# Attention and channel-mix block on one core: the shift of the softmax transposed by DMA, four operand buffers, and the turns of input and attention in 64-row tiles with one copy

## The chip, the cores and the metric

The kernel runs on one core of a Trainium2 chip. The metric is device microseconds of one execution, the median of several runs. TensorE (PE in the rows) multiplies and transposes, VectorE (DVE), ScalarE (ACT) and GpSimd (POOL) do the elementwise work, and SyncE (SP) issues all DMAs, in the order of its program.

## What is computed

Input x is (32, 256, 128) fp32. For each of 32 batches:

```python
xn = layernorm(x)
q, k, v = xn @ wq + bq, xn @ wk + bk, xn @ wv + bv      # 16 heads of 8
att = softmax(q @ k.T / sqrt(8)) @ v                    # per head, 256 x 256 scores
xp = xn shifted down one token, zeros first
r = sigmoid((mu_r*xn + (1-mu_r)*xp) @ W_r)
k2 = square(relu((mu_k*xn + (1-mu_k)*xp) @ W_k))
y = x + att.reshape(256, 128) @ wo.T + bo + r * (k2 @ W_v)
```

## The kernel before

A batch is one step t; its 16 heads are 16 units u. A step of the program works on several batches at once: the layernorm of batch t+4 and t+3, the projections of t+3, the spill of t+2, the maxima of t+1, the exponentials of t, and the output of t-1. `live(d)` says that batch t+d exists, `n(d)` is the count that a semaphore has when batch t+d is done. Each engine has its own program in order of time, and semaphores tie them. The steps 4 to 27 are a loop of 4 steps a pass (`LOOP`), the rest is straight code.

The scores are made twice from split operands. q and k are cut into three bf16 parts (h, m, l), written to DRAM (`spill`) and read back as `ops`, where 48 rows hold 6 products of parts. Rows 0 to 63 and 64 to 127 of `ops` hold different heads (r = 0, 1), so that TensorE runs two matmuls at once, in two tiles of 64 rows. The first time (line 717) VectorE takes the maximum of each row from the bank (line 557); the second time (line 707) three more rows of `ops` (51 in all) carry the negated maximum in three bf16 parts against ones, so that the bank holds score minus maximum and ScalarE takes the exponential (line 454). Line 717 runs two units ahead (`LEAD`): at unit 14 it starts with batch t+2. A bank for exponentials is free again two units later.

The way of the maximum, the *shift*, for each half of the heads: GpSimd splits it into three parts (`split_max`, lines 332 to 339), TensorE transposes them (`transpose_shift`, line 639: half 1 in unit 1 of its own step, half 0 of batch t+1 in unit 9), ScalarE copies them from PSUM (`move_shift`, line 424), SyncE copies them into `ops` (`load_shift`, line 257). Half 0 is needed at unit 0, half 1 at unit 8.

After the units 1, 5, 9 and 13 stand 16 value matmuls in four column tiles (`mix_values`, line 631). After the other odd units stand full fp32 matmuls: unit 3 the gate (736) and the transposes of the mixed values (747), from which VectorE takes the reciprocals (567) and `att` (570); unit 7 the channel mix (758), the transposes of xn (768) and of att (773), which ScalarE copies to `xn_t` (472) and, with the bias bv added, to `att_t` (476); unit 11 the values (646), the hidden layer (792) and the output projection (799); unit 15 the projections K and Q (665, 673). Two banks, `misc[0]` and `misc[1]`, take turns in all of these as `near` and `far`. VectorE adds the gate to the channel mix at line 584; GpSimd adds ffn and x (`rest`, line 376) and the output (407).

SyncE's step: load x of batch t+4, `load_ops` half 1 of t+1, spill h, `load_shift` half 1, spill m and l, `load_ops` half 0 of t+2 when the scores of unit 7 have been read, `load_shift` half 0, store y of t-1. `ops` has two buffers.

## Time and profile before

| | |
|---|---|
| median of 3 runs | 468.71 us (468.67 to 470.33) |
| the profiled execution | 468.32 us, its span 466.2 us |
| busy share | PE 96%, DVE 86%, ACT 85%, POOL 79%, weight loads (PEld) 59% |
| DMA engines | 45% of the span, 60.4 MB |
| mean granted TensorE clock | 0.971; 1.00 (2.4 GHz) in each stretch read from 40 us on, 0.50 to 0.60 from 14 to 40 us |

The span runs from the first to the last instruction; the execution's own time has some 2 us around it. The times of the rows below are microseconds from the span's start. PE is a matmul or transpose, PEld a weight load; an fp32 matmul is two passes and so two instructions, a transpose is one. The length of a TensorE row includes the way through the array, so that starts, not ends, show its pace.

### The profile page before, as it was taken

What the parts mean: (1) busy time and instruction counts of PE and PEld (TensorE: products, weight loads), DVE (VectorE), ACT (ScalarE), POOL (GpSimd) and SP (SyncE); (2) the same over time, 40 slices, a digit from 0 to 9 for tenths busy, and PEclk for the clock granted to TensorE, in tenths of its full rate; (3) what the DMA queues carried; (4) which work ended last, traced back from release to release, by engine and by line L of the source; (5) the groups of instructions that cost most, each with busy time, mean ns of one, the idle gap of its engine ahead of it and who ended that gap; (6) DMA issues with size and microseconds to landing.
All of it is one profiled execution on the core that took longest, in us unless ns stands there. A gap on an engine that the chain in (4) does not pass through costs nothing.

```text
span 466.2 us, 15769 instructions
## 1 busy us (share of the span) xinstructions
PE 449.2 (96%) x5254; PEld 275.1 (59%) x5254; DVE 400.7 (86%) x824; ACT 394.1 (85%) x896; POOL 366.5 (79%) x674
## 2 busy tenths in 40 slices
PE   6689999999999999999999999999999999999996
PEld 5245666666656666556665666566656666666554
DVE  7578999999988999899999999899998999989831
ACT  2138899999988999989998999989998999989894
POOL 6667888888888988888888888888888888887321
PEclk9558999999999999999999999999999999999999
DMA  4533465545345545344554544355545444455100
GB/s 135 158 116 99 124 162 148 142 134 150 109 140 148 157 127 155 108 132 130 148 159 129 156 139 127 104 147 155 159 137 138 136 126 125 137 151 147 51 15 24
DMA packets 86061, 60.43 MB, mean 130 GB/s; under 512 B 6224, under 2 KB 73808, under 8 KB 86032
## 3 DMA queue, kind: packets, MB, share of 16 engines
q1 hardware_dynamic: 86032, 60.06, 45.0%
q8 instruction: 17, 0.28, 0.3%
q14 instruction: 12, 0.10, 0.1%
HBM read 29.89 MB, written 29.36 MB: 127 GB/s over the span
## 4 chain that ended last, share of the span: by engine, by line
PE 88%; DMA 3%; issue 2%; DVE 2%; ACT 2%; SPq 1%; ACTq 0%; DVEq 0%; POOL 0%
PE bank_val L631 26%; PE bank_exp L707 18%; PE bank_max L717 11%; PE misc L736 5%; PE misc L758 4%; PE misc L646 4%; PE misc L665 3%; PE misc L747 3%; PE misc L799 3%; PE misc L792 3%; PE misc L673 2%; PE misc L773 2%; PE misc L768 1%; DMA ops<-spill 1%; DVE neg_max L557 1%
## 5 line engine op out<-in xcount | busy, mean ns | idle before, releaser
L557 DVE TENSOR_REDUCE neg_max<-bank_max 128x2 f32<-128x512 f32 x512 | 327.9, 684 | 37.9 <-PE bank_max L717 32.8
L454 ACT ACTIVATE probs<-bank_exp 128x512 f32<-128x512 f32 x504 | 273.5, 597 | 27.4 <-PE bank_exp L707 25.3
L717 PE MATMUL bank_max<-ops 48*128 48x256 bf16 x1024 | 161.5, 278 | 0.0
L707 PE MATMUL bank_exp<-ops 51*128 51x256 bf16 x1008 | 156.0, 273 | 4.2 <-issue 2.1
L631 PE MATMUL bank_val<-probs,val 128*25 128x256 f32 x2048 | 136.8, 385 | 0.8 <-ACT probs L454 0.8
L707 PEld LDWEIGHTS bank_exp<-ops 51*128 51x128 bf16 x1008 | 74.7, 95 | 66.2 <-issue 51.5
L631 PEld LDWEIGHTS bank_val<-probs,val 128*25 128x25 f32 x2048 | 50.5, 103 | 52.2 <-issue 27.0
L717 PEld LDWEIGHTS bank_max<-ops 48*128 48x128 bf16 x1024 | 77.0, 96 | 5.7
L356 POOL TENSOR_SCALAR xn<-x_in,moments,rstd 128x128 f32<-128x128 f32 x62 | 49.3, 802 | 0.0
L395 POOL TENSOR_TENSOR mixed_x<-mixed_x,xn_t 128x512 f32<-128x512 f32 x32 | 40.7, 1273 | 2.5
L370 POOL TENSOR_TENSOR qk_l<-qk_rest,qk_m 128x512 bf16<-128x512 f32 x31 | 36.0, 1163 | 2.5
L523 DVE SCALAR_TENSOR_TENSOR qk_rest<-misc,col,qk_h 128x256 f32<-128x256 f32 x64 | 30.6, 479 | 6.2 <-ACT qk_h L436 6.2
L391 POOL TENSOR_TENSOR mixed_x<-dx,col 128x512 f32<-128x512 f32 x32 | 33.4, 1042 | 2.5
L436 ACT ACTIVATE qk_h<-misc,col 128x256 bf16<-128x256 f32 x64 | 27.2, 480 | 8.9 <-PE misc L665 7.0
L407 POOL TENSOR_TENSOR y<-projected,rest 128x256 f32<-128x256 f32 x31 | 22.6, 729 | 14.2 <-ACT projected L491 14.2
L366 POOL TENSOR_TENSOR act_sq<-act_r 128x256 f32<-128x256 f32 x32 | 19.6, 613 | 17.0 <-DVE qk_rest L523 17.0
L424 ACT COPY shift<-misc 24x256 bf16<-24x256 bf16 x64 | 23.2, 362 | 9.1 <-PE misc L639 2.5
L351 POOL TENSOR_TENSOR x_bo<-x_in,bo_all 128x256 f32<-128x256 f32 x32 | 23.2, 726 | 4.1 <-issue 3.9
L402 POOL TENSOR_TENSOR rstd<-var_eps,minus_half 128x2 f32<-128x2 f32 x32 | 22.8, 712 | 2.5
L646 PE MATMUL misc<-w,xn_t 128*128 128x128 f32 x128 | 23.1, 304 | 1.3 <-DVE qk_rest L523 1.3
L665 PE MATMUL misc<-xn_t,w 128*128 128x256 f32 x64 | 23.4, 449 | 1.0 <-ACT xn_t L472 1.0
L472 ACT COPY xn_t<-misc 128x256 f32<-128x256 f32 x32 | 12.0, 374 | 14.0 <-PE misc L768 13.9
(77 smaller groups left out, 627.9 us busy)
## 6 DMA issues: line engine op xcount, KB each, us to landing
ops<-spill SPq DMA_DIRECT2D x126, 192.0 KB, 3.4
spill<-qk_h SPq DMA_DIRECT2D x64, 192.0 KB, 3.3
spill<-qk_m SPq DMA_DIRECT2D x64, 128.0 KB, 1.9
x_in<-x SPq DMA_DIRECT2D x32, 128.0 KB, 2.2
spill<-qk_l SPq DMA_DIRECT2D x32, 128.0 KB, 1.8
y_out<-y SPq DMA_DIRECT2D x32, 128.0 KB, 1.9
ops<-shift SPq DMA_DIRECT2D x128, 6.0 KB
w<-weights SPq DMA_DIRECT2D x1, 448.0 KB, 3.0
```

Source lines behind the costliest of these rows:

```text
L356: last = nc.gpsimd.tensor_scalar(xn[:, i, :], x_in[(c + 3) % TURN][:, i, :], moments[:, i, 0:1], rstd[:, i:i + 1], ALU.subtract, ALU.mult)
L370: nc.gpsimd.tensor_tensor(qk_l[:, :, :], qk_rest[:, :, :], qk_m[:, :, :], ALU.subtract).then_inc(l_done, 1)
L391: nc.gpsimd.tensor_tensor(mix[:, :, :], dx[:, :].unsqueeze(1).broadcast_to([P, 2, S]), col[:, C_MUR:C_MUK + 1].unsqueeze(2).broadcast_to([ ...
L395: nc.gpsimd.tensor_tensor(mix[:, :, :], mix[:, :, :], prev.unsqueeze(1).broadcast_to([P, 2, S]), ALU.add).then_inc(mix_tokens_done, 1)
L454: nc.scalar.activation(probs[g % 2][:, u % G, :, :], exp_bank(u, live)[:, :, :], ACT.Exp, scale=SCALE).then_inc(exp_done[u], 1)
L523: nc.vector.scalar_tensor_tensor(out=qk_rest[:, a, :], in0=bank[:, 0:S], scalar=col[:, C_BQ + a:C_BQ + a + 1], in1=qk_h[:, a, :], op0=ALU. ...
L557: nc.vector.tensor_reduce(out=neg_max[hf][:, :, r, pr], in_=bank_max[MAX_BANK[v]][:, :, :], axis=AX_X, op=ALU.max, negate=True).then_inc(m ...
L631: last = nc.tensor.matmul(bank_val[SW * j:SW * j + MW, g // 2, :], weights[:, 0:MW] if fresh else weights[:, VW:VW + MW], probs[g % 2][:, ...
L646: last = nc.tensor.matmul(bank[:, i * D:(i + 1) * D], xn_t[c % TURN][:, 1 + i * P:1 + (i + 1) * P], w[:, W_V, :], start=True, stop=True)
L665: nc.tensor.matmul(far[:, 0:S], w[:, W_K, :], moving, start=True, stop=True).then_inc(qk_psum[1], 1)
L707: exp_mm = nc.tensor.matmul(exp_bank(u, live)[:, i, :], ops[p][rows, hf, 1, pr, i * P:(i + 1) * P], ops[p][rows, hf, 0, pr, :], start=True ...
L717: max_mm = nc.tensor.matmul(bank_max[MAX_BANK[v]][:, i, :], of[rows, max_hf, 0, max_pr, i * P:(i + 1) * P], of[rows, max_hf, 1, max_pr, :] ...
```

## The change

- **Shift.** `max_parts` becomes 128 columns wide, with zeros behind the 24 that are used. SyncE transposes it by a DMA transpose into `shift` (`transpose_shift`), and copies the 24 rows that count into `ops` as before. TensorE's line 639 and ScalarE's line 424 go. GpSimd's split of half 0 moves ahead of `rest` (line 376).
- **Operand buffers.** `ops` has four buffers instead of two. Both halves of batch t+2 are loaded in step t, half 0 after the transpose of the shift of half 0, half 1 after the copy of that shift. The ones of the two new buffers are copied by DMA from the first (`copy_ones`). 
- **SyncE's order.** Transpose of half 1, spill h, shift of half 1, spill m and l, transpose of half 0, ops half 0, shift of half 0, ops half 1, and last the load of x (of batch t+5) and the store of y.
- **Turns.** xn and att are transposed in tiles of 64 rows: eight transposes with 64 columns in place of four with 128, the upper rows into bank 0 of `misc` and the lower into bank 1, all in the columns S to 2S. The wait for `att_done`, which stood before the transposes of att, stands before the last matmul of line 758. One ScalarE copy of 128x512 takes both results into `xn_t`, which has twice the columns; `att_t` is its second half.
- **Bias.** bv is no longer added to `att_t`; one matmul at the start forms bv @ wo and VectorE adds it to bo.
- **Loop.** The loop covers steps 4 to 23.

The diff, cut to its core (left out: the declarations of semaphores, the bias, and waits that only follow the renaming of `misc`):

```diff
-LOOP = (1, 7)
+LOOP = (1, 6)
...
-        xn_t = [sb(f"xn_t{i}", [P, 1 + S]) for i in range(TURN)]
+
+        xn_t = [sb(f"xn_t{i}", [P, 1 + 2 * S]) for i in range(TURN)]
...
-        ops = [sb(f"ops{i}", [P, 2, 2, PR, S], BF16) for i in range(2)]
+        ops = [sb(f"ops{i}", [P, 2, 2, PR, S], BF16) for i in range(TURN)]
...
-        max_parts = [sb(f"max_parts{i}", [P, ST, 2, 3, PR], BF16) for i in range(2)]
-        shift = [sb(f"shift{i}", [2 * 3 * PR, S], BF16) for i in range(2)]
...
+        max_parts = [sb(f"max_parts{i}", [P, ST, P], BF16) for i in range(2)]
+        shift = [sb(f"shift{i}", [P, ST, P], BF16) for i in range(2)]
...
-        misc = [psum(f"misc{i}", [P, 2 * S]) for i in range(2)]
+
+        misc = psum("misc", [P, 2, 2 * S])
...
+            def copy_ones():
+
+                sp.wait_ge(k_filled[0], 1)
+                for i in range(2, TURN):
+                    for r in range(2):
+                        rows = slice(RG * r + KS, RG * r + KE)
+                        sp.dma_start(ops[i][rows, :, 1], ops[0][rows, :, 1]).then_inc(ones_in, 16)
...
-            def load_shift(half, p, count, before):
-
-                after(sp, shift_done[half], count)
...
+            def transpose_shift(half, count, before):
+                sp.wait_ge(parts_zero, 1)
+                sp.wait_ge(max_split[half], count)
+                after(sp, shift_in[half], before)
+                sp.dma_start_transpose(shift[half][:, :, :], max_parts[half][:, :, :].rearrange("p n c -> p (n c)")).then_inc(
+                    shift_done[half], 16)
+
+            def load_shift(half, c, done, before):
+
+                sp.wait_ge(shift_done[half], done)
                 after(sp, shift_in[half], before)
                 for r in range(2):
-                    sp.dma_start(ops[p][RG * r + KS:RG * r + KE, half, 0],
-                                 shift[half][3 * PR * r:3 * PR * (r + 1), :]).then_inc(shift_in[half], 16)
+                    sp.dma_start(ops[c][RG * r + KS:RG * r + KE, half, 0],
+                                 shift[half][3 * PR * r:3 * PR * (r + 1), :, :]).then_inc(shift_in[half], 16)
...
             def step(t, c, n, moved, paired, quad, live):
                 p = c % 2
-                if live(4) and live(0):
-
-                    sp.wait_ge(x_bo_done, n(0))
-                    sp.wait_ge(xn_done, n(0))
-                    load_x(t + 4, c)
-                if live(1):
-
-                    after(sp, exp_scores[H - 1], n(-1))
-                    load_ops(1, 1 - p, moved(1, SPILLS), moved(0, 2))
+                if live(0):
+                    transpose_shift(1, n(0), moved(-1, 2))
                 if live(2):
...
-                    load_shift(1, p, n(0), moved(-1, 2))
+                    load_shift(1, c, moved(0, 1), moved(-1, 2))
                 if live(2):
                     spill_part(p, "m", qk_m, (m_done, m_done), n)
                     spill_l(p, n)
-
-                    after(sp, exp_scores[HALF - 1], n(0))
+                if live(1):
+                    transpose_shift(0, n(1), moved(0, 2))
+                if live(2):
+
+                    after(sp, exp_scores[H - 1], n(-1))
                     if not live(0):
                         sp.wait_ge(k_filled[p], 1)
                     if live(1):
-                        load_ops(0, p, moved(2, SPILLS), moved(1, 2))
+                        load_ops(0, (c + 2) % TURN, moved(2, SPILLS), moved(1, 2))
                     else:
-                        load_first_ops(p, moved(2, SPILLS))
+                        load_first_ops((c + 2) % TURN, moved(2, SPILLS))
                 if live(1):
-                    load_shift(0, 1 - p, n(1), moved(0, 2))
+                    load_shift(0, (c + 1) % TURN, moved(1, 1), moved(0, 2))
+                if live(2):
+                    load_ops(1, (c + 2) % TURN, moved(2, SPILLS), moved(1, 2))
+                if live(1) and not live(0):
+                    copy_ones()
+                if live(5) and live(1):
+                    sp.wait_ge(x_bo_done, n(1))
+                    sp.wait_ge(xn_done, n(1))
+                    load_x(t + 5, (c + 1) % TURN)
                 if live(-1):
-
-                    sp.wait_ge(y_done, n(-1))
-                    sp.dma_start(out_dram[t - 1], y[1 - p][:, :].rearrange("p (n d) -> p n d", n=ST)).then_inc(
-                        out_done[1 - p], 16)
-
-            steps(sp, step, (2, SPILLS))
+                    store_y(t - 1, 1 - p, n(-1))
+
+            steps(sp, step, (1, 2, SPILLS))
...
                                             ALU.subtract).then_inc(l_done, 1)
+                if live(1):
+                    split_max(0, n(1), moved(0, 1))
                 if live(-1):
                     pool.wait_ge(ffn_done, n(-1))
                     after(pool, y_done, n(-3))
...
-            def move_shift(half, bank, count, before):
-                act.wait_ge(shift_psum[half], count)
-                after(act, shift_in[half], before)
-                nc.scalar.copy(shift[half][:, :], shift_in_bank(bank)).then_inc(shift_done[half], 1)
...
-                    if u == 1 and live(0):
-                        move_shift(1, near, n(0), moved(-1, 2))
...
-                        move_values(p, far, n(2))
-                    if u == 7 and live(3):
-                        act.wait_ge(xn_t_psum, n(3))
-                        nc.scalar.copy(xn_t[(c + 3) % TURN][:, 1:1 + S], near[:, S:2 * S]).then_inc(xn_t_done, 1)
-                    if u == 7 and live(-1):
-                        act.wait_ge(att_t_psum, n(-1))
-                        after(act, wo_psum, n(-2))
-                        nc.scalar.activation(att_t[:, :], far[:, 0:S], ACT.Identity,
-                                             bias=col[:, C_BV:C_BV + 1]).then_inc(att_t_done, 1)
-                    if u == 9 and live(1):
-                        move_shift(0, far, n(1), moved(0, 2))
+
+                        for r in range(2):
+                            act.wait_ge(xn_t_psum[r], n(3))
+                        move_values(p, near, n(2))
+                    if u == 7 and (live(3) or live(-1)):
+                        turned = xn_t[(c + 3) % TURN]
+
+                        after(act, ffn_psum, n(0))
+                        for r in range(2):
+                            after(act, xn_t_psum[r], n(3))
+                            after(act, att_t_psum[r], n(-1))
+
+                        cols = slice(0 if live(3) else S, 2 * S if live(-1) else S)
+                        nc.scalar.copy(turned[:, 1 + cols.start:1 + cols.stop].rearrange("p (n r c) -> p r n c", r=2, c=RG),
+                                       misc[:, :, S + cols.start // 2:S + cols.stop // 2].rearrange(
+                                           "p r (n c) -> p r n c", c=RG)).then_inc(xn_t_done if live(3) else att_t_done, 1)
...
-            def transpose_shift(half, bank):
-                for st in range(ST):
-                    last = nc.tensor.transpose(shift_in_bank(bank)[:, st * P:(st + 1) * P],
-                                               max_parts[half][:, st].rearrange("p r j k -> p (r j k)"),
-                                               ident16[:, :])
-                last.then_inc(shift_psum[half], 1)
...
-                    if u == 1 and live(0):
-                        pe.wait_ge(max_split[1], n(0))
+                    if u == 3 and live(0):
                         pe.wait_ge(act_r_done, n(0))
                         after(pe, qk_rest_done[1], n(2))
-                        transpose_shift(1, near)
-                    if u == 3 and live(0):
-                        pe.wait_ge(shift_done[1], n(0))
...
                     if u == 5 and live(0):
                         mix_values(0, n(0), n(-1), p)
+                    if u == 7 and live(2) and not live(1):
+                        pe.wait_ge(qk_rest_done[1], n(2))
+                        project_values(c + 2, near)
+                    if u == 7 and live(3):
+                        pe.wait_ge(xn_done, n(3))
+                        after(pe, qk_rest_done[0], n(2))
+                        after(pe, qk_rest_done[1], n(2))
                     if u == 7 and live(0):
                         pe.wait_ge(act_sq_done, n(0))
                         pe.wait_ge(gate_done, n(0))
                         for i in range(ST):
+                            if i == ST - 1:
+
+                                after(pe, att_done, n(-1))
                             last = nc.tensor.matmul(near[:, i * D:(i + 1) * D], act_sq[:, i * P:(i + 1) * P],
                                                     w[:, W_VV, :], start=True, stop=True)
                         last.then_inc(ffn_psum, 1)
-                    if u == 7 and live(2) and not live(1):
-                        pe.wait_ge(qk_rest_done[0], n(2))
-                        project_values(c + 2, far)
                     if u == 7 and live(3):
-                        pe.wait_ge(xn_done, n(3))
-                        after(pe, qk_rest_done[1], n(2))
                         for i in range(ST):
-                            last = nc.tensor.transpose(near[:, S + i * P:S + (i + 1) * P], xn[:, i, :], ident[:, :])
-                        last.then_inc(xn_t_psum, 1)
+                            for r in range(2):
+                                rows, k = slice(RG * r, RG * (r + 1)), S + i * RG
+                                last = nc.tensor.transpose(misc[:, r, k:k + RG], xn[rows, i, :], ident[rows, rows])
+                                if i == ST - 1:
+                                    last.then_inc(xn_t_psum[r], 1)
                     if u == 7 and live(-1):
-                        pe.wait_ge(att_done, n(-1))
+                        if not live(0):
+                            pe.wait_ge(att_done, n(-1))
                         for st in range(ST):
-                            last = nc.tensor.transpose(far[:, st * P:(st + 1) * P],
-                                                       att[:, st * H:(st + 1) * H].rearrange("p k e -> p (k e)"),
-                                                       ident[:, :])
-                        last.then_inc(att_t_psum, 1)
+                            for r in range(2):
+                                rows, k = slice(RG * r, RG * (r + 1)), S + (ST + st) * RG
+                                last = nc.tensor.transpose(misc[:, r, k:k + RG],
+                                                           att[rows, st * H:(st + 1) * H].rearrange("p k e -> p (k e)"),
+                                                           ident[rows, rows])
+                                if st == ST - 1:
+                                    last.then_inc(att_t_psum[r], 1)
                         if not live(0):
                             keep_running(2)
                     if u == 9 and live(0):
                         mix_values(1, n(0), n(-1), p)
-                    if u == 9 and live(1):
-                        pe.wait_ge(max_split[0], n(1))
-                        after(pe, att_t_done, n(-1))
+                    if u == 11 and live(1) and live(0):
+                        if live(3):
+                            pe.wait_ge(xn_t_done, n(3))
+                        elif live(-1):
+                            pe.wait_ge(att_t_done, n(-1) - (B - TURN))
                         after(pe, qk_rest_done[0], n(2))
-                        if not live(0):
-                            pe.wait_ge(consts_made, 2)
```

## Rows read from the trace of the kernel before

**Rows 1.** Page, chain that ended last: shares of the span by engine.
```profile
PE 88%; DMA 3%; issue 2%; DVE 2%; ACT 2%; SPq 1%; ACTq 0%; DVEq 0%; POOL 0%
```

**Rows 2.** Stretch; busy us of PE, PEld, DVE, ACT, POOL; clock, DMA share, GB/s.
```profile
200.00:213.26 13.26, 13.26 (x165) 8.27 (x164) 12.05 (x26) 12.21 (x29) 11.45 (x21) 1.00 0.52 146
```

**Rows 3.** TensorE in order of time: start us, us, engine, line, operation, tiles, count.
```profile
200.71 0.28 PE L707 MATMUL bank_exp<-ops 51*128 51x256 bf16 x1
...
201.25 1.07 PE L631 MATMUL bank_val<-probs,val 128*25 128x256 f32 x16
...
202.34 0.28 PE L707 MATMUL bank_exp<-ops 51*128 51x256 bf16 x1
...
204.95 1.06 PE L631 MATMUL bank_val<-probs,val 128*25 128x256 f32 x16
205.95 0.28 PE L707 MATMUL bank_exp<-ops 51*128 51x256 bf16 x1
...
212.89 0.71 PE L758 MATMUL misc<-w,act_sq 128*128 128x128 f32 x4
213.44 0.38 PE L768 MATMUL misc<-ident,xn 128*128 128x128 f32 x2
213.66 0.38 PE L773 MATMUL misc<-ident,att 128*128 128x128 f32 x2
213.97 0.28 PE L707 MATMUL bank_exp<-ops 51*128 51x256 bf16 x1
```

**Rows 4.** VectorE in order of time, same batch.
```profile
206.41 1.29 DVE L557 TENSOR_REDUCE neg_max<-bank_max 128x2 f32<-128x512 f32 x2 [0.25 <-PE bank_max L717]
207.86 0.48 DVE L523 SCALAR_TENSOR_TENSOR qk_rest<-misc,col,qk_h 128x256 f32<-128x256 f32 x1 [0.16 <-ACT qk_h L436]
...
209.84 2.71 DVE L557 TENSOR_REDUCE neg_max<-bank_max 128x2 f32<-128x512 f32 x4
212.47 0.35 DVE L567 RECIPROCAL inv_den<-misc 128x32 f32<-128x32 f32 x1
212.86 0.42 DVE L570 TENSOR_TENSOR att<-misc,inv_den 128x256 f32<-128x256 f32 x1
```

**Rows 5.** Groups of instructions by form: busy, mean ns.
```profile
L454 ACT ACTIVATE probs<-bank_exp 128x512 f32<-128x512 f32 x504 | 273.5, 597 | 27.4 <-PE bank_exp L707 25.3
...
L639 PE MATMUL misc<-ident,max_parts 128*24 128x128 bf16 x128 | 17.8, 221 | 0.0
...
L758 PEld LDWEIGHTS misc<-w,act_sq 128*128 128x128 f32 x128 | 16.7, 190 | 6.7 <-issue 6.7
...
L768 PEld LDWEIGHTS misc<-ident,xn 128*128 128x128 f32 x64 | 8.2, 148 | 1.5 <-DVE xn L531 0.8 <-issue 0.4 <-POOL xn L356 0.3
```

**Rows 6.** All engines near the end of the span, in order of time.
```profile
461.16 0.42 DVE L570 TENSOR_TENSOR att<-misc,inv_den 128x256 f32<-128x256 f32 x1
461.64 0.20 PEld L773 LDWEIGHTS misc<-ident,att 128*128 128x128 f32 x2 [0.21 <-DVE att L570]
```

**Rows 7.** ScalarE in order of time, units 7 to 9.
```profile
213.86 0.37 ACT L472 COPY xn_t<-misc 128x256 f32<-128x256 f32 x1
214.13 0.48 ACT L476 ACTIVATE att_t<-misc,col 128x256 f32<-128x256 f32 x1
214.49 1.09 ACT L454 ACTIVATE probs<-bank_exp 128x512 f32<-128x512 f32 x2
```

**Rows 8.** GpSimd in order of time: the last step of a split.
```profile
207.13 0.22 POOL L339 TENSOR_TENSOR max_parts<-max_rest,max_parts 128x16 bf16<-128x16 f32 x1
```

**Rows 9.** SyncE's DMA issues in order of time.
```profile
209.68 1.53 SPq L257 DMA_DIRECT2D ops<-shift  x2
...
214.33 0.80 SPq L242 DMA_DIRECT2D ops<-spill  x2
```

**Rows 10.** Page, DMA issues: KB each, median us from issue to landing.
```profile
ops<-spill SPq DMA_DIRECT2D x126, 192.0 KB, 3.4
...
spill<-qk_l SPq DMA_DIRECT2D x32, 128.0 KB, 1.8
```

More of the change, by code:

```diff
@@ L327, in split_max @@
                 m, zero = neg_max[half], zeros[:, :, :, :]
-                part = [max_parts[half][:, :, :, j, :] for j in range(3)]
+                parts = max_parts[half][:, :, 0:2 * 3 * PR].rearrange("p n (r j k) -> p n r j k", r=2, j=3)
+                part = [parts[:, :, :, j, :] for j in range(3)]
                 last_unit = HALF * (half + 1) - 1
                 after(pool, max_done[last_unit], count)
-                after(pool, shift_psum[half], before)
+                after(pool, shift_done[half], before)
                 nc.gpsimd.tensor_tensor(part[0], m[:, :, :, :], zero, ALU.add).then_inc(max_h[half], 1)
@@ L440, in step @@
                 p = c % 2
-                near, far = misc[p], misc[1 - p]
+                near, far = misc[:, p, :], misc[:, 1 - p, :]
                 if live(2):
@@ L502, in _ @@
             nc.vector.memset(zeros[:, :, :, :], 0.0)
+            for i in range(2):
+                last = nc.vector.memset(max_parts[i][:, :, :], 0.0)
+            last.then_inc(parts_zero, 1)
             nc.vector.memset(eps[:, :], EPS)
@@ L613, in _ @@
             for _ in range(WARM):
-                nc.tensor.matmul(misc[0][:, 0:P], ident[:, :], ident[:, :], start=True, stop=True)
+                nc.tensor.matmul(misc[:, 0, 0:P], ident[:, :], ident[:, :], start=True, stop=True)
             def keep_running(count):
@@ L676, in step @@
                 p = c % 2
-                near, far = misc[p], misc[1 - p]
+                near, far = misc[:, p, :], misc[:, 1 - p, :]
                 for u in range(H):
```

89 lines of the change are left out of this document (51 added, 38 removed).

## Prediction

> **What bounds the kernel now.** I read the chain of waits first: 88% of it is TensorE's [rows 1]. Then one steady batch (200.71 to 213.97 us, 13.26 us, as the others of the loop body): TensorE is busy without a hole, VectorE for 12.05 us and ScalarE for 12.21 us of it [rows 2]. So TensorE's order of work is the period, and a batch has only 1.2 us in which VectorE is idle: whatever is taken from TensorE helps up to there and no further, and whatever new wait ties TensorE to VectorE costs at once.
>
> Third, TensorE in order of time [rows 3]. Three things are to be seen. (a) The bf16 shift transposes, two per half, are cheap: 16 value matmuls start at 201.25, two transposes follow, the next score matmuls start at 202.34, 1.09 us later; where none stand between (204.95 to 205.95) it is 1.00. A pair of them costs 0.09 us. (b) The block at the end of unit 7 (line 758, then 768 and 773) runs from 212.89 to 213.97. Two transposes start in 0.22 (213.44, 213.66), so one each 0.11 us; four 758 passes in 0.55, so they stream from 213.00 on, after a load of 0.11. (c) Two units of scores are four starts of 0.11, but take 0.54 to the next block (200.71 to 201.25): 0.10 goes into the change of tile size, and with the load that can't be made ahead it is 0.20 before line 758. Going back is 0.09 (213.66 and two transposes of 0.11 end at 213.88; the scores start at 213.97).
>
> Fourth, VectorE beside it [rows 4]. From its reduce at 206.41 VectorE is busy, but for 0.16 us, till att is written at 212.86+0.42 = 213.28 us. That chain begins with the scores of unit 14 (TensorE, 205.95) and everything in it is VectorE's own work. TensorE's first transpose of att starts at 213.66, so today att is ready 0.3 us early.
>
> **The change, part by part.**
>
> *Shift transposes leave TensorE* (line 639: 128 in all, 4 a batch [rows 5]). Two pairs of 0.09 us. The pair in unit 1 stands between unit 14 and unit 7, where, as the next part shows, TensorE will wait for VectorE anyway: worth nothing then. The pair in unit 9 is worth 0.09 us.
>
> *The wait for att_done moves ahead of the last 758 matmul.* The new transposes write columns S and up of both banks of misc, also those that VectorE still reads for att; so the wait stands before the matmul of i=1 and thus before its weight load. Today that load starts at 213.11. att is ready at 213.28, and a load starts 0.06 us after att where TensorE waits for it alone (461.16+0.42 to 461.64) [rows 6]; I allow 0.06 to 0.12. The load starts at 213.34 to 213.40 instead of 213.11: 0.23 to 0.29 us of stall against the old place, and the 0.09 of unit 1 is already lost in it, since VectorE's chain hangs on unit 14 and not on the shift transposes. I take 0.26. Queued behind the wait: the last ffn matmul, all eight transposes, the scores of units 8 and 9. ScalarE, VectorE's ffn (line 584) and so y wait for those.
>
> *Eight transposes of 64 rows in place of four of 128.* Old block: 4 x 0.11 plus 0.09 back to row tiles, 0.53 us. New: the switch comes before the transposes (0.09 to 0.20) and none after, since the scores have row tiles too. Each moves 64 columns, half of 0.11. If a pair of row tiles runs together, 4 pairs x 0.055 = 0.22. The weight loads have 128 columns still. A transpose's load takes 148 ns against 190 for one of line 758 [rows 5], so its streaming part should be some 0.05 shorter than the 0.11 that a load has in today's stream: in sequence 8 x 0.055 = 0.44, at the very worst 8 x 0.11 = 0.88. New block 0.31 to 0.64 (0.97 to 1.08 at the worst); I take 0.45, a gain of 0.08, since nothing in the rows says that loads of two row groups exclude each other and nothing that they don't (bounds: gain 0.22, loss 0.11; the worst is a rival).
>
> The Trainium skill speaks on both sides here. TensorEngine Tiling, Key Properties: a change of tiling mode drains the engine, and tiles can load and multiply in parallel; the gaps of 0.20 and 0.09 us agree with the first, and by the second the block would be at its lower end. TensorE: Matmul & The Clock Gate, section LDWEIGHTS, says that a load's time depends on its columns and not on its rows, so that halving the rows makes no load cheaper; with loads in sequence this gives the upper end.
>
> *One copy on ScalarE instead of two, and no shift copies.* Now xn_t is copied at 213.86 and att_t at 214.13, and the exps of units 8 and 9 start at 214.49 [rows 7], 0.52 us after their scores were started. The new copy (128x512) needs the last transpose. That ends about 0.22 us after its start (the 0.27 of a full one less half its columns), so the copy starts 0.2 us after the start of the scores of unit 8, holds ScalarE 0.49 us (what one of two exps of the same size takes of their 1.09, the last being 0.60 long [rows 5]), and the exps end at 0.2+0.49+1.09 = 1.79 us after that start. Unit 11's scores need that bank; their natural start is 0.54+1.00 (units 8 and 9, then the value matmuls without line 639) + 0.22 (unit 10) = 1.76 us after it [rows 3], and the wait needs about 0.1. Stall 0.13 us (0 to 0.25). Before: 0.52+1.09 = 1.61, no stall. The removed shift copies (line 424, in units 9 and 1) come after this point, so they don't help here; elsewhere ScalarE isn't late.
>
> *The shift by DMA.* No row shows a DMA transpose. Half 1: GpSimd ends its split at 207.13+0.22 = 207.35 [rows 8]; SyncE can issue the transpose at 207.4, ahead of the spills of h. Call X the time from issue to landing. Then two ops<-shift issues (1.53 us for two [rows 9]) and the landing of the second; nearest row, 1.8 us for a 128 KB spill [rows 10]. 207.4 + X + 0.77 + 1.8 must not pass unit 8 at 213.97 plus the 0.2 that the change itself adds: hidden while X is under 4.2 us. Half 0: its split no longer waits behind rest (line 376), and is done at about 213.8 (att's half reduce ends near 212.5, four GpSimd steps of 0.3); needed at unit 0, 220.8+0.2: hidden while X is under 4.6. For X the nearest rows are 1.8 us and 3.4 us (ops<-spill, 192 KB [rows 10]), plus up to 0.8 of issue; I take 3. Cost nothing, cover 1.2 us; without cover every us of X is a us per batch.
>
> *SyncE's order.* The load of ops half 0 for batch t+2 goes out at 214.33 now [rows 9], when the l spill has landed. The transpose of half 0 is issued at 213.8 before it; at 0.77 us of issue the load is 0.25 late and lands 3.4 after 215.0, 218.4; needed at unit 14, 219.2. Hidden, 0.8 spare. Half 1 of ops goes out one batch earlier than now, which the four buffers allow; input and output go last, and a batch of SyncE holds some 9 us of issues and has 4 of spare. The ones copied into two more buffers, the bias sum made once by a matmul, and the loop with one pass less and four straight batches more: once each, no path that lasts; nothing.
>
> **Sum.** Per batch +0.26 -0.09 -0.08 +0.13 = +0.22 us. From t=1 to 31, 31 batches: +6.8 us. The profiled execution took 468.32 us (span 466.2), so 475.1; the median is 468.71, 0.4 above it, less than I can resolve. Bounds of the same sum: 0.23-0.09-0.22+0 = -0.08, and 0.29-0.09+0.11+0.25 = +0.56 a batch: 466 to 485.7.
>
> **The rivals.**
> *Nothing stalls and the removed work shows (faster).* Place: the att_done wait. If VectorE ends att before 213.0 (a reduce or the att pair 0.3 us earlier), then both 0.09 and the block's 0.08 count, and ScalarE's stall with its 0.13 might stay away: -0.26 a batch, 460 us (to 455.5 at the lower end of the block). For it: VectorE has 1.2 us of idle time a batch. Against it: from 206.41 on it has 0.16.
> *The terms cancel.* Transposes in pairs at full speed and no ScalarE stall: -0.05, 467 us; "same".
> *The transpose lands late (slower still).* X of 5 us: unit 8 waits 0.8 us a batch, which takes up the later waits for att (VectorE catches up meanwhile) but is itself larger: about +0.8 x 31 = 25, some 493 us. For it: SyncE waits for the landing with the spills of m and l queued behind it. Against: 1.2 us of cover at X of 3. The Trainium skill, VectorE: DVE Perf Modes, section on the three transpose paths, gives 1309 ns for a 128x128 bf16 transpose by DMA; two of them would be 2.6 us as an estimate, under the bound. No run here shows it yet.
> *The DMA transpose disturbs the other transfers*, and ops half 0 lands 1.1 us late at unit 14, 0.3 more than is spare: 0.3 a batch more, 484. *The eight loads go in sequence at 0.11 each*: the block is 0.97 instead of 0.45, +0.52 a batch, 491; today's loads are hidden behind matmuls as long as they are, so the rows can't exclude it.
>
> **Chances.** The sum as made 0.50 (own range 470.7 to 484); cancel 0.15; faster 0.22; late or disturbing transposes and loads in sequence together 0.13. The likeliest time is 475. Measurements of this kernel resolve about 0.5% (2.3 us). Faster by over 0.5% 0.22, within it 0.15, slower 0.63. The range 462 to 488 leaves out the fast half of the faster case and most of these last.
>
> **What the profile would show.** Line 639 gone; a stall of about 0.3 us before the second matmul of line 758, put down to VectorE's att, in every steady batch; unit 8 at once behind the eight transposes, their block 0.3 to 0.6 us; the 128x512 copy at about 0.6 us and a small wait of unit 11 for the exps; no wait of the scores for ops<-shift. The period of line 758 near 13.48 in place of 13.26. I am wrong if that period is under 13.26 (att is earlier than I think), or if units 0 or 8 wait for a DMA.

## The result, and the profile after

The changed kernel takes 481.18 us (median of 4 runs, 478.7 to 481.95); the kernel before, beside it, 469.25 us (468.67 to 470.33). The ratio is 1.0255, with a 95% interval of 1.0223 to 1.0288: slower by 11.9 us, where I had forecast 6.3. The profiled execution took 481.16 us (span 479.3; before 468.32 and 466.2). Some executions of one and the same kernel take over 1.5% longer than its fastest; the ratios in this text leave them out, the medians do not.

The chain that ended last, and the DMA issues (KB each, median us to landing), on the page of the changed kernel:

```profile
PE 87%; issue 4%; DVE 3%; ACT 2%; DMA 2%; SPq 1%; POOL 0%; DVEq 0%; ACTq 0%; POOLq 0%
...
ops<-spill SPq DMA_DIRECT2D x126, 192.0 KB, 3.5
...
spill<-qk_l SPq DMA_DIRECT2D x32, 128.0 KB, 1.9
...
shift<-max_parts SPq DMA_TRANSPOSE x64, 2.4
```

TensorE still leads the chain, but "issue" (time for which the profile names no releaser) has doubled against [rows 1]. The landing of the ops loads has hardly moved (3.5 against 3.4 [rows 10]), and the DMA transpose lands after 2.4 us, inside my bound of 4.2.

One undisturbed batch of the changed kernel (stretch; busy us of PE, PEld, DVE, ACT, POOL; clock, DMA share, GB/s), then TensorE in it, in order of time:

```profile
233.58:246.93 13.35, 13.33 (x165) 7.80 (x163) 12.29 (x26) 11.60 (x26) 11.51 (x21) 1.00 0.52 148
```
```profile
233.58 0.93 PE L795 MATMUL misc<-w,act_sq 128*128 128x128 f32 x4
234.44 0.34 PE L802 MATMUL misc<-ident,xn 64*128 64x64 f32 x4
234.62 0.29 PE L811 MATMUL misc<-ident,att 64*128 64x64 f32 x4
234.74 0.27 PE L738 MATMUL bank_exp<-ops 51*128 51x256 bf16 x1
...
235.28 1.06 PE L665 MATMUL bank_val<-probs,val 128*25 128x256 f32 x16
...
236.28 0.28 PE L738 MATMUL bank_exp<-ops 51*128 51x256 bf16 x1
236.40 0.27 PE L738 MATMUL bank_exp<-ops 51*128 51x256 bf16 x1
236.69 0.28 PE L738 MATMUL bank_exp<-ops 51*128 51x256 bf16 x1
```

The granted clock is full (2.4 GHz, as in [rows 2]) and the batch is 13.35 us long against 13.26: only 0.09 more, where I had 0.22. So the regular part of the loss is 30 x 0.09 = 2.7 us. The rest is irregular. Over all batches I took the start of unit 14's scores less the start of the 16 value matmuls ahead of them, less the undisturbed 1.00 us [rows 3]: these stalls add up to 1.5 us in the kernel before and 12.5 us in the changed one (batches 0 to 30). 6.2 us of them lie in batches 0 to 7, 4.8 in batches 24 to 29, 1.5 in the sixteen between. From the ffn matmuls (the channel mix, line 758 before and 795 after) of batch 0 to those of batch 30 the two kernels differ by 13.2 us (414.8 against 401.6), and 2.7 + 11.0 makes 13.7. (The last batch of each pass of the loop takes 0.4 to 0.7 us longer in the kernel before, without a stall at unit 14, and about as much in the changed one.)

What unit 14 waits for shows in SyncE's DMA issues. First in the undisturbed batch, then in batch 25 (ffn matmuls at 383.35), with TensorE there:

```profile
233.22 0.36 SPq L281 DMA_DIRECT2D spill<-qk_l  x1
234.51 1.21 SPq L265 DMA_TRANSPOSE shift<-max_parts  x1
235.83 0.98 SPq L243 DMA_DIRECT2D ops<-spill  x2
```
```profile
384.28 1.79 SPq L265 DMA_TRANSPOSE shift<-max_parts  x1
386.92 0.80 SPq L243 DMA_DIRECT2D ops<-spill  x2
```
```profile
390.88 0.27 PE L738 MATMUL bank_exp<-ops 51*128 51x256 bf16 x1 [0.97 <-issue]
```

The loads of ops half 0 (line 243) go out 2.25 us after the ffn matmuls of unit 7; before, 1.44 (214.33 [rows 9] less 212.89 [rows 3]). They wait behind the transpose of half 0, which is held for GpSimd's split until 0.93 and then takes 1.21 us to issue. Unit 14 comes 4.24 us after their issue in undisturbed batches; there the loads take about 4 us from the first issue to the landing of the second (4.2 in the mean of the loop's batches), so the slack is 0.2 us or less. In the kernel before it was 4.88 less 4, 0.9. The row of unit 14 names no releaser, but the landings in the trace do: in both kernels each of its stalls of 0.05 us or more ends 0.09 us after the last part of the two loads has landed. In the changed kernel the loads are issued late in nine batches (2.4 to 4.5 us after the ffn matmuls), which hold 8.3 of the 12.5 us; batch 25 is one, and unit 14 starts 390.88 - 386.92 = 3.96 us after the issue. In most of the others with a stall the issue is on time and the landing is late, up to 5.2 us after it.

SyncE's waits (us in total, times, longest), first in the kernel before, then in the changed one, say the same of the issue: the l spill's landing, which held the ops loads before, has given way to the wait for max_parts.

```profile
SPq L194 <- DMA spill<-qk_l: 48.5, 32, 2.9
```
```profile
SPq L195 <- POOL max_parts L362: 33.3, 44, 2.1
...
SPq L273 <- DMA shift<-max_parts: 9.3, 14, 1.5
...
SPq L195 <- DMA spill<-qk_l: 5.9, 8, 1.5
```

### The profile page after: what moved, and what is told of

The parts are those of the page before. It is cut to its first block, busy times and chain, and to the rows that moved or that the text cites. A ratio compares the mean times of both kernels' runs of the same rounds, so it can differ in the third digit from the quotient of the medians.

```text
span 479.3 us, 15771 instructions
## 1 busy us (share of the span) xinstructions
PE 449.4 (94%) x5256; PEld 261.1 (54%) x5256; DVE 401.3 (84%) x826; ACT 374.5 (78%) x804; POOL 367.6 (77%) x674
## 4 chain that ended last, share of the span: by engine, by line
PE 87%; issue 4%; DVE 3%; ACT 2%; DMA 2%; SPq 1%; POOL 0%; DVEq 0%; ACTq 0%; POOLq 0%
PE bank_val L665 26%; PE bank_exp L738 19%; PE bank_max L748 10%; PE misc L795 6%; PE misc L763 4%; PE misc L673 4%; PE misc L692 4%; PE misc L774 3%; PE misc L838 3%; PE misc L828 3%; PE misc L700 2%; PE misc L802 2%; DVE neg_max L582 2%; ACT probs L474 1%; DMA ops<-spill 1%
## 5 line engine op out<-in xcount | busy, mean ns | idle before, releaser
L738 PE MATMUL bank_exp<-ops 51*128 51x256 bf16 x1008 | 159.6, 272 | 14.7 <-issue 11.5
L748 PE MATMUL bank_max<-ops 48*128 48x256 bf16 x1024 | 165.3, 277 | 0.0
L748 PEld LDWEIGHTS bank_max<-ops 48*128 48x128 bf16 x1024 | 75.6, 96 | 4.8
L500 ACT COPY xn_t<-misc 128x512 f32<-128x512 f32 (+1 forms) x36 | 19.7, 547 | 31.0 <-PE misc L811 17.2
L432 POOL TENSOR_TENSOR y<-projected,rest 128x256 f32<-128x256 f32 x31 | 22.7, 731 | 12.5 <-ACT projected L514 12.5
L795 PE MATMUL misc<-w,act_sq 128*128 128x128 f32 x128 | 29.4, 324 | 0.0
L355 POOL TENSOR_TENSOR max_parts<-neg_max,zeros 128x16 bf16<-128x16 f32 x64 | 14.1, 220 | 16.1 <-DVE neg_max L582 13.2
L795 PEld LDWEIGHTS misc<-w,act_sq 128*128 128x128 f32 x128 | 18.9, 188 | 11.2 <-issue 6.7
```

What stands on the lines that cost most here:

```text
L738: exp_mm = nc.tensor.matmul(exp_bank(u, live)[:, i, :], ops[c][rows, hf, 1, pr, i * P:(i + 1) * P], ops[c][rows, hf, 0, pr, :], start=True ...
L748: max_mm = nc.tensor.matmul(bank_max[MAX_BANK[v]][:, i, :], of[rows, max_hf, 0, max_pr, i * P:(i + 1) * P], of[rows, max_hf, 1, max_pr, :] ...
L795: last = nc.tensor.matmul(near[:, i * D:(i + 1) * D], act_sq[:, i * P:(i + 1) * P], w[:, W_VV, :], start=True, stop=True)
```

## The experiments

"Period" below is the time from one batch's ffn matmuls to the next in undisturbed batches of the loop (a range where hardly one is undisturbed), "unit 14" the sum of its stalls as above, both of the profiled execution; the ratio is to the kernel before that ran beside it, with its 95% interval. The groups of runs stood on different chips, so that between groups ratios compare better than medians.

| kernel | median us | ratio | period | unit 14 |
|---|---|---|---|---|
| before | 468.3 to 469.3 | | 13.26 | 1.5 |
| after | 481.18 | 1.0255 [1.0223, 1.0288] | 13.35 | 12.5 |
| ops_first | 556.3 | 1.1873 [1.1825, 1.1921] | 14 to 17 | 23.3 |
| loop7 | 480.34 | 1.0271 [1.0229, 1.0313] | 13.35 | 8.1 |
| loop4 | 487.59 | 1.0381 [1.0319, 1.0443] | 13.35 | 16.3 |
| before_loop4 | 469.88 | 1.0029 [0.9999, 1.0058] | 13.26 | 7.3 |
| tensor_shift | 474.12 | 1.0126 [1.0093, 1.0158] | 13.44 | 4.3 |
| spare_ahead | 497.33 | 1.0621 [1.0571, 1.067] | 13.6 to 14.0 | 24.4 |
| spare_behind | 469.06 | 1.002 [0.9989, 1.005] | 13.26 | 2.9 |
| att_wait | 480.64 | 1.0252 [1.0208, 1.0295] | 13.16 to 13.3 | 17.1 |
| half1_dma | 478.24 | 1.0119 [1.0044, 1.0194] | 13.35 | 7.8 |
| tensor_att | 466.97 | 0.9954 [0.9931, 0.9977] | 13.22 | 4.3 |
| half1_dma_att | 468.44 | 0.9997 [0.9967, 1.0028] | 13.13 | 7.6 |
| tensor_att_loop7 | 465.11 | 0.9938 [0.9916, 0.996] | 13.22 | 2.5 |
| half1_att_loop7 | 467.93 | 0.9988 [0.9962, 1.0015] | 13.13 | 4.3 |

**ops_first**: in SyncE's step the transpose of half 0 moves behind the ops loads.

```diff
-                if live(1):
-                    transpose_shift(0, n(1), moved(0, 2))
                 if live(2):
...
                         load_first_ops((c + 2) % TURN, moved(2, SPILLS))
                 if live(1):
+                    transpose_shift(0, n(1), moved(0, 2))
                     load_shift(0, (c + 1) % TURN, moved(1, 1), moved(0, 2))
```


> The changed kernel, but SyncE issues the loads of ops half 0 before the DMA transpose of shift half 0. My theory: of the 12 us that the change cost, some 10 are irregular stalls of unit 14 (12.5 us over all batches, against 1.5 in the kernel before), which come because the 1.2 us issue of the transpose stands ahead of the ops loads and leaves them no slack. Then unit 14's stalls fall to about 2 us and the time to 470 to 473 us, with the regular period still at 13.35 us. Rival 1: the loads land late because the DMA transpose and its many small packets hold the DMA engines; moving the issue changes little, 478 to 482 us. Rival 2: the 1.2 us only moves to half 0 of the shift, which then lands late at unit 0: stalls appear there and the time stays near 479 us or more.

556.3 us: my theory's number fell and rival 2 happened, far beyond its price. SyncE in order of time:

```profile
224.47 0.80 SPq L243 DMA_DIRECT2D ops<-spill  x2
225.37 1.21 SPq L265 DMA_TRANSPOSE shift<-max_parts  x1
228.53 1.51 SPq L273 DMA_DIRECT2D ops<-shift  x2
230.14 0.83 SPq L243 DMA_DIRECT2D ops<-spill  x2
231.22 0.41 SPq L228 DMA_DIRECT2D x_in<-x  x1
231.84 0.41 SPq L292 DMA_DIRECT2D y_out<-y  x1
233.49 1.22 SPq L265 DMA_TRANSPOSE shift<-max_parts  x1
```

The transpose's landing (3.2 us here), which in the changed kernel passes while the ops loads are issued, is now a wait of SyncE with everything queued behind it: from 226.58 to 228.53 it issues nothing, and the next batch's spills are late by that. Over the whole run SyncE's wait for that landing has grown from 9.3 us in the changed kernel to 90.2, and TensorE's scores wait for the shift, as rival 2 says:

```profile
SPq L273 <- DMA shift<-max_parts: 90.2, 59, 3.7
```
```profile
PE bank_exp L737 <- DMA ops<-shift: 47.7, 49, 2.8
```

SyncE's chain of issues and landings has become the period, 14 to 17 us. Taking 0.8 us from one wait put two landings in sequence.

**loop7, loop4, before_loop4**: only the number of batches in the loop changes (in loop7 x is loaded at the start of SyncE's step, for batch t+4).

```diff
-LOOP = (1, 6)
+LOOP = (1, 7)
...
+                if live(4) and live(0):
+                    sp.wait_ge(x_bo_done, n(0))
+                    sp.wait_ge(xn_done, n(0))
+                    load_x(t + 4, c)
                 if live(0):
                     transpose_shift(1, n(0), moved(-1, 2))
...
-                    load_x(t + 5, (c + 1) % TURN)
```
That is loop7; loop4 and before_loop4 have only `LOOP = (1, 4)`.


> The changed kernel with the loop of the kernel before (passes 1 to 6 instead of 1 to 5), so that four batches fewer are written out in straight code; the load of x moves to the start of SyncE's step, for a batch one earlier, to allow it. Theory (late ops loads, set off by fetches of instructions for straight code): the stalls of unit 14 in batches 24 to 27, 3.0 us together, go: about 478 us. Rival (the irregular stalls have nothing to do with straight code): no change within 0.3%, 480 to 482 us.

> The changed kernel with two passes of the loop fewer, so that eight batches more are straight code. Theory: each straight batch costs the changed kernel some 0.75 us of stall at unit 14, so about +6 us: 487 us. Rival (straight code costs nothing by itself): no change, 480 to 482 us.

> The kernel before with three passes of the loop fewer, so that twelve batches more are straight code. Theory: the fetches of instructions come here too, but the loads of ops half 0 have 0.8 us of slack, which covers most of what they delay: under +2.5 us, 469 to 471.5 us. Rival (a straight batch costs 0.75 us by itself, whatever the order on SyncE): +9 us, 478 us.

loop4 costs what the theory said (+6.4 us), and its unit 14 stalls in batches 16 to 23, now straight code, are 6.8 us in its profiled execution, the slowest of four; in the changed kernel the same batches had 0.7. The kernel before bears twelve more straight batches for 1.6 us, with an interval of the ratio that includes no change (0.9999 to 1.0058); its profile, with 7.3 us at unit 14, is of one of its slowest executions (472.78 us). loop7 missed: 480.34 us lies in the rival's range. In its profiled execution, the fastest of four (478.4 us), the stalls of batches 24 to 27 fall from 3.0 to 0.4 us, but batches 9 to 23 keep 0.1 to 0.3 in about half of them and the median moves by 0.8 us only, less than I can tell. What differs between straight code and loop is seen in the DMA view of single microseconds of the changed kernel. This is 384 to 385, in batch 25, while the l spill, issued at 382.99, is on its way:

```profile
## 3 DMA queue, kind: packets, MB, share of 16 engines
q1 hardware_dynamic: 201, 0.10, 30.6%
q8 instruction: 1, 0.02, 9.5%
```

A packet of 16 KB of instructions is fetched about every 10 us of straight code and of the loop's first pass, and holds one of the 16 DMA engines for 0.9 to 1.6 us (9.5% of 16 engines for 1 us is 1.5); packets of 8 KB come between, of 0.3 to 0.8 us. In the changed kernel there are none from 139 to 364 us, and there the stalls are small. The landings of the l spill in the 15 profiles, from 60 us on, make the tie close: 348 spills met no fetch, and every one landed 1.8 to 2.1 us after its issue; 47 had a 16 KB packet on its way meanwhile and took 3.3 us in the median, up to 4.1 (25 with only an 8 KB packet: 2.0, up to 2.7). In batch 25 it is 3.9. What the traces can't tell is in the open points below.

**tensor_shift**: the changed kernel with both shifts on TensorE and ScalarE again; turns, buffers and SyncE's order stay.

```diff
-                if live(1):
-                    transpose_shift(0, n(1), moved(0, 2))
...
+                    if u == 9 and live(1):
+                        pe.wait_ge(max_split[0], n(1))
...
+                        transpose_shift(0, far)
```


> The changed kernel with both shifts made by TensorE and ScalarE again, as before; the 64-row turns with one copy, the four operand buffers and SyncE's new order stay. Theory: the loads of ops half 0 go out 1.4 us after the start of the ffn matmuls of unit 7 again (2.25 in the changed kernel), so the irregular stalls of unit 14 fall from 12.5 us to about 2, while the regular period rises from 13.35 to some 13.44 us (the pair of bf16 transposes in unit 9 is back): 473 to 475 us. Rival (the stalls come from SyncE's new order or the buffers, not from the DMA transpose): they stay, 482 to 485 us.

474.12 us: as the theory said, though unit 14 keeps 4.3 us where I had 2. This splits the change: everything but the shift (the 64-row turns with one copy, the buffers, SyncE's order, the loop) costs 5 us (469.1 to 474.1), most of it in the period, which is 0.18 us longer; the shift by DMA costs 7 (to 481.2), though it takes TensorE's period from 13.44 to 13.35. The ops loads go out at 1.44 again and unit 14 follows 5.06 us later.

**spare_ahead, spare_behind**: the kernel before, with a DMA transpose of a spare tile that nobody reads.

```diff
+            def spare_transpose(spilled, before):
+                sp.wait_ge(spare_zero, 1)
+                after(sp, spill_done, spilled)
+                after(sp, spare_done, before)
+                sp.dma_start_transpose(spare_out[:, :], spare_in[:, :]).then_inc(spare_done, 16)
...
                     spill_l(p, n)
 
+                    spare_transpose(moved(2, SPILLS), moved(1, 1))
                     after(sp, exp_scores[HALF - 1], n(0))
```
That is spare_ahead; in spare_behind the call stands behind `load_ops` and `load_first_ops` of half 0.


> The kernel before with one DMA transpose more per batch, 128x128 bf16 of a spare tile that nobody reads, issued by SyncE right ahead of the loads of ops half 0. Theory: its issue (0.6 to 0.8 us as an estimate: the 128x256 one took 1.21) takes the 0.9 us of slack that those loads had, and unit 14 gets irregular stalls as in the changed kernel: 476 to 482 us, with the period otherwise 13.26 us. Rival (the order on SyncE doesn't matter; what matters is something else in the change): 469 to 471 us.

> The same spare DMA transpose in the kernel before, but issued right behind the loads of ops half 0, so that the traffic is the same and the loads go out as before. Theory: under +2 us, 469 to 471.5 us. Rival (the transpose's traffic slows the landing of the ops loads, wherever it is issued): as spare_ahead, 476 to 482 us.

The cleanest pair: the same traffic costs 28 us ahead of the ops loads, 23 of them at unit 14, and nothing behind them. The mechanism stood; my size for spare_ahead was too small, since half the tile does not issue in half the time. SyncE and TensorE of spare_ahead:

```profile
201.01 1.13 SPq L267 DMA_TRANSPOSE spare_out<-spare_in  x1
202.26 0.98 SPq L245 DMA_DIRECT2D ops<-spill  x2
```
```profile
206.43 0.27 PE L719 MATMUL bank_exp<-ops 51*128 51x256 bf16 x1 [0.48 <-issue]
```

1.13 us of issue and the gap behind it move the loads by 1.25 us, past the slack of 0.9, and behind a transpose the two loads take 0.98 us to issue and not 0.80 [rows 9]: now every batch of the loop stalls 0.4 to 0.8 us at unit 14, here 4.17 us after their issue.

**att_wait**: the wait for att behind the last ffn matmul, ahead of the transposes.

```diff
                         for i in range(ST):
-                            if i == ST - 1:
-
-                                after(pe, att_done, n(-1))
...
+                    if u == 7 and live(0):
+                        pe.wait_ge(ident_made, 1)
+                        after(pe, att_done, n(-1))
```


> The changed kernel, but TensorE waits for att behind the last ffn matmul of unit 7, right ahead of the 64-row transposes. Theory: the stall in the ffn matmuls (0.22 us a batch against its own place) falls to some 0.05 to 0.1, because a matmul and its load fit into it: period 13.35 to some 13.22 us, total -3 to -5 us: 476 to 478 us. Rival: the wait of unit 11 for the exps takes over what is won, as everything from unit 8 on starts earlier but ScalarE's copy and exps are what it waits for: no change, 480 to 482 us.

480.64 us, no change, but not through the rival that I had named: unit 14 now stalls 0.1 to 0.4 us in nearly every loop batch. What TensorE gains before it comes to unit 14 it loses there, because the ops loads are issued at 2.26 as before. The late loads were next to be the bound of the whole loop, with 0.2 us to spare.

**half1_dma, tensor_att, half1_dma_att**: half 0 through TensorE, half 1 through the DMA; tensor_shift with att_wait's edit; both. half1_dma against tensor_shift:

```diff
+                if live(0):
+                    transpose_shift(1, n(0), moved(-1, 2))
...
-                    if u == 1 and live(0):
-                        move_shift(1, near, n(0), moved(-1, 2))
...
-                        transpose_shift(1, near)
```


> The changed kernel with the shift of half 0 made by TensorE and ScalarE again (unit 9), while half 1 stays on the DMA's transpose, which SyncE issues ahead of the spills of h. Theory: only the transpose that stands ahead of the loads of ops half 0 does harm; the one of half 1 has cover, so unit 14 stalls as little as without any DMA transpose (4 us or less over all batches) and the pair of bf16 transposes gone from unit 1 wins nothing, because TensorE waits for att afterwards: 472.5 to 475 us. Rival (any DMA transpose on SyncE's queue delays the chain of spills and ops loads): unit 14's stalls come back in part, 477 to 481 us.

> The kernel tensor_shift (474.1 us, period 13.44) with the wait for att behind the last ffn matmul. In att_wait this freed some 0.2 us a batch, which the late ops loads took back (unit 14 waited 0.15 to 0.2 us in nearly every batch). Theory: here the loads have 1.1 us of slack, so the gain shows: period 13.24 to 13.30, 468 to 470.5 us. Rival (the rest of unit 11's wait for the exps or VectorE's reduces take it): 473 to 475 us.

> Both: half 0 by TensorE, half 1 by the DMA's transpose, and the wait for att behind the last ffn matmul. Theory: the 0.09 us of the pair in unit 1 counts now, at least in part, as TensorE waits less for att: period 13.15 to 13.25 us, 465 to 469 us, the first version that may beat the kernel before. Rival (VectorE's chain to att sets the block in either case, so the pair in unit 1 still wins nothing): as tensor_att.

half1_dma scatters (471.3 to 481.96 us), so its ratio says little. My theory for it did not hold: the median, 478.24, lies in the rival's range, unit 14 stalls for 7.8 us where I allowed 4, and the period is 13.35, so that the pair gone from unit 1 wins 0.09 after all. The ops loads go out at 1.65 instead of 1.44: the transpose of half 1 pushes the spills behind it by 0.2 us. tensor_att beats its forecast and, by 0.5%, the kernel before. TensorE in its batch:

```profile
225.61 0.71 PE L804 MATMUL misc<-w,act_sq 128*128 128x128 f32 x4
226.26 0.34 PE L814 MATMUL misc<-ident,xn 64*128 64x64 f32 x4
226.43 0.29 PE L823 MATMUL misc<-ident,att 64*128 64x64 f32 x4
226.55 0.27 PE L746 MATMUL bank_exp<-ops 51*128 51x256 bf16 x1
```

The ffn matmuls run without a hole, and from their start to the scores of unit 8 it is 0.94 us: 1.16 in the changed kernel, 1.08 before (212.89 to 213.97 [rows 3]). half1_dma_att has the shortest period of all, 13.13, and gives it back at unit 14 (7.6 us, nearly all in straight code and the loop's first pass); its 468.44 us are within my range, but do not beat the kernel before.

**tensor_att_loop7, half1_att_loop7**: both with the loop of the kernel before, by loop7's edit.


> tensor_att (466.97 us) with four batches fewer in straight code, as in loop7. Theory (irregular stalls of unit 14 belong to straight code, where fetches of instructions delay the spills and loads): batches 24 to 27 lose their 1.3 us of stalls: 465 to 466.3 us. Rival (they belong to those places in time, whatever the code): no change, 466.5 to 467.5 us.

> half1_dma_att (468.44 us, period 13.13) with four batches fewer in straight code. Theory: its batches 24 to 27 had 2.2 us of stalls at unit 14, and in the loop it has none, with 0.6 us of slack: about -2.2 us, 465.5 to 467 us. Rival: no change, 467.5 to 469 us.

The first does what the theory says in its profile: batches 24 to 27 without a stall. It takes 465.11 us, 0.6% below the kernel before (interval 0.9916 to 0.996); that it is faster than tensor_att isn't shown, since the intervals of the two ratios overlap. The second lost its stalls there too (2.2 to 0.1 us), but its loop got new ones of 0.1 to 0.2 us in four batches, in each of which the ops loads went out at 2.5. The load of x now stands ahead of the transpose of half 1 on SyncE; that this is the reason was not tried. Its median, 467.93, lies in the rival's range and moved by 0.5 us, within the noise.

## Why the prediction was wrong, and what of it held

**SyncE's order** is the step that failed: "Hidden, 0.8 spare" for the loads of ops half 0 was wrong, and the rival beside it, at 0.3 a batch and 484 us, came nearest in total but had another cause. Three things were wrong in it. I let the transpose issue in 0.77 us, what a 6 KB DMA takes; it takes 1.21. I counted 0.25 us of delay; it is 0.81, that is 0.25, 0.44 for the longer issue and 0.11 for the gap behind it, and the first ops load behind the transpose then takes 0.51 us to issue where it took 0.32. And I treated what was left as cover that costs nothing, though the kernel before used up the same slack in places: its unit 14 already stalled 0.93 us in batch 7. With 0.2 us left, each disturbance of the chain from the l spill to the ops landing goes through to TensorE: 11 us. spare_ahead and spare_behind show that it is the place on the queue and not the traffic, which also speaks against the rival that the transposes disturb other transfers: in the loop the second ops load lands 3.6 us after its own issue with them and without them (tensor_shift). SyncE's issues take 10.2 us a batch in the changed kernel, where I had some 9.

**att_done wait**: forecast 0.26 us a batch against the old place, the pair of unit 1 included. Measured: 1.16 less the 0.94 of tensor_att, 0.22 with the wait against none, and 0.13 when the 0.09 that the missing pair of unit 1 gives back is taken off. In the batch shown above the load of the second ffn matmul starts 0.05 us after att is written (233.97 to 234.02). Right in kind, twice too large, because the pair of unit 1 is not "worth nothing": leaving it out took the period from 13.44 to 13.35 (tensor_shift to half1_dma). From unit 14's scores to att written it is 7.24 us in the changed kernel (240.07 to 247.31) and 7.33 before (205.95 [rows 3] to 213.28 [rows 4]); "Everything in it is VectorE's own work" was the wrong reading: [rows 4] merge four reduces into one row of 2.71 us, and between the second and the third of them VectorE waits 0.15 us, till 211.27, for the scores that TensorE makes in unit 4 (done at 211.20), and these stand behind the pair of unit 1. Without the pair it waits 0.07.

**The pair of unit 9**: forecast 0.09, measured nothing (half1_dma and the changed kernel both have 13.35). TensorE waits for the exps at unit 11 and waits the shorter for it.

**Eight transposes**: forecast a gain of 0.08 with the bound at 0.22; measured 0.14 (0.94 against 1.08). The eight take 0.30 us (234.44 to 234.74), 0.075 a pair with the way back, so loads of two row groups do run together, and the rival of loads in sequence, 0.97 us, is refuted. The Trainium skill, TensorEngine Tiling (Array Packing), Key Properties, says that tiles can load and multiply in parallel; by that rule I had given the block its lower end, and the trace agrees.

**ScalarE's copy**: forecast 0.13 us at unit 11. The scores of unit 11 start 0.29 us after the second start of unit 10 (236.40 to 236.69) where 0.12 is usual: 0.17, of which 0.09 only replaces the pair of unit 9 (with the pair, in tensor_shift, it is 0.20). So 0.08 is new.

**The shift's landing**: X of 2.4 us against 3 taken; no wait of units 0 or 8, as forecast. The Trainium skill, VectorE: DVE Perf Modes, the three transpose paths, has 1309 ns for a 128x128 transpose, from which I had estimated 2.6 us for two of them. Issue to landing is 2.4, but that the numbers are near is luck: the 128x128 one of spare_ahead lands 2.2 us after its issue, so one is not half of two, and of either time the issue alone is 1.1 to 1.2. The page has no figure for what SyncE spends on the issue, which was what counted.

The terms as measured, -0.09 (pair of unit 1) + 0.22 - 0.14 + 0.08, come to +0.07 of the +0.09 that the period shows. So the regular part was 2.7 us and not 6.8, and a term counted as nothing brought 11. That 481.2 lies in the range from 462 to 488 is luck: it came from a regular part that I had put too high by 4 us and an irregular one that I had not put in at all.

What stays open: every late l spill had an instruction packet on its way, and the stalls move with the straight code (loop4, tensor_att_loop7), but no run took the fetches away while keeping the code, so that they cause the delays is argued, and how they would is unknown. The stalls of 0.1 to 0.5 us in the changed kernel's loop come without any fetch, from landings 4.3 to 4.6 us after the issue; in the loop of the kernel before they scatter from 3.7 to 4.3, and unit 14 comes at 4.9. Why half1_dma scatters by 10 us wasn't tried.

## What to carry to other kernels

Cost a DMA that is put into a queue by its issue time from a row of its own kind, and compare the delay with the slack of the next load on that queue: the time from its issue to its first use, less the same time in a batch where the use really waits. A slack of a few tenths of a microsecond is no cover: read how often the kernel before already overran it. And when an edit of TensorE shows no gain, look for the load whose issue didn't move with it; here one and the same edit gave nothing clear of noise beside the late loads (att_wait, 0.5 us) and 7.2 us beside early ones (tensor_att).

## What the runs showed of the hardware

- A DMA transpose costs SyncE about the same at the two sizes tried: 1.21 us for 128x256 bf16, 1.13 for 128x128 (plain issues of 192 KB take 0.3 to 0.5 each, the first behind a transpose 0.5). It lands in 2.4 and 2.2 us, and the larger one in 3.2 behind two ops loads (ops_first).
- fp32 transposes of 64 rows on two row groups run in pairs: four pairs and the way back to the scores take 0.30 us.
- Instruction fetches use the same 16 DMA engines as the kernel's own transfers, one of them for 0.9 to 1.6 us for each 16 KB. A 128 KB spill lands in 1.8 to 2.1 us without one and in 3.3 (median) with one on its way.
